# A graph network's tail on one core: the last batch's first 128 columns taken ahead of the rest, with TensorE's order behind them rewritten

## The reference, cut to what matters

```python
# x [16, 512, 128], adj [16, 512, 512]
def L0(x, mask):                       # per batch
    xc = transpose(x)
    h = relu(bn(conv1d(xc, conv1_w)))
    h = bn(conv1d(h, conv2_w, taps=17))
    x_conv = transpose(relu(h + xc))
    s = x @ w_se.T + b_se
    A = exp(-dist(s, s)) * mask        # 512 x 512
    x_nmp = A @ relu(x @ w_msg.T + b_msg)
    gi = concat(x_conv, x_nmp) @ w_ih.T + b_ih
    gh = x @ w_hh.T + b_hh
    r = sigmoid(gi_r + gh_r); z = sigmoid(gi_z + gh_z)
    n = tanh(gi_n + r * gh_n)
    return (1 - z) * n + z * x
def L1(x, adj):                        # five groups of the first 25 nodes
    for g, idx in enumerate(GROUPS):   # sizes 25, 9, 7, 6, 6
        An = normalised(adj[:, idx][:, :, idx])
        h = relu(An @ (x[:, idx] @ W1[g]) + b1[g])          # 128 -> 256
        out_g = relu(An @ (h @ W2[g]) + b2[g])              # 256 -> 128
        fused[:, idx] += softmax(fusion_w)[g] * out_g
    return fused
x = layernorm(x + L0(x, adj))
x = layernorm(x + L1(x, adj))          # L1 is 0 from node 25 on
```

## Time and profile before

| what | value |
|---|---|
| median of 3 runs | 358.56 us |
| profiled execution | 357.92 us |
| its span | 356.1 us |
| TensorE busy | 340.6 us (96%) |
| VectorE busy | 318.2 us (89%) |
| ScalarE busy | 236.7 us (66%) |
| GpSimd busy | 95.0 us (27%) |
| the chain that ended last, by engine | TensorE 77%, VectorE 10%, ScalarE 5%, issue 4% |
| landing of a store of `yoo`, from issue | 2.3 us |

### The profile page before, as it was taken

The page is one execution under the profiler, slowest core; times in us unless marked ns, Lnnn a source line. Parts: engine busy times, 40 slices in busy tenths (PEclk is TensorE's granted clock), DMA queues, the critical chain, the costliest instruction groups (busy, mean ns, idle before and its releaser), DMA issues.

```text
span 356.1 us, 6267 instructions
## 1 busy us (share of the span) xinstructions
PE 340.6 (96%) x1790; PEld 277.0 (78%) x1790; DVE 318.2 (89%) x562; ACT 236.7 (66%) x409; POOL 95.0 (27%) x153
## 2 busy tenths in 40 slices
PE   4989999999999999999999999999999999999894
PEld 1567678976889688977998788968897798866673
DVE  2999999999999999999999899999999999896526
ACT  4382665748856696748674885669684876876760
POOL 4770001503050504131050505040222206062023
PEclk9999999999999999999999999999999999999998
DMA  6914332514043312604161404412260415301101
GB/s 178 327 24 122 111 112 50 165 31 148 24 128 124 101 49 66 206 0 147 39 204 29 147 17 121 135 59 88 55 203 14 147 33 178 96 12 36 29 2 53
DMA packets 30950, 33.95 MB, mean 95 GB/s; under 512 B 4884, under 2 KB 18124, under 8 KB 30932
## 3 DMA queue, kind: packets, MB, share of 16 engines
q1 hardware_dynamic: 30166, 33.55, 31.4%
q10 hardware_dynamic: 766, 0.18, 0.2%
HBM read 24.85 MB, written 4.40 MB: 82 GB/s over the span
## 4 chain that ended last, share of the span: by engine, by line
PE 77%; DVE 10%; ACT 5%; issue 4%; DMA 2%; SPq 0%; DVEq 0%; POOLq 0%; ACTq 0%; POOL 0%
PE p_outer L669 18%; PE ring L669 15%; PE p_middle L669 14%; PE p_r L669 9%; PE p_z L669 8%; PE p_gi L669 6%; PE p_gh L669 5%; PE ring L748 2%; DMA cst<-consts 2%; DVE am L1331 1%; ACT am_h L1101 1%; ACT yoo L1083 1%; ACT ac L376 1%; DVE gtn L1337 1%; ACT he L373 1%
## 5 line engine op out<-in xcount | busy, mean ns | idle before, releaser
L1232 POOL TENSOR_TENSOR base<-mv,vscale 128x4 f32<-128x4 f32 x16 | 5.1, 319 | 235.3 <-DVE mv L1363 235.3
L669 PE MATMUL p_outer<-t_h,w_h 128*128 128x344 f32 x131 | 41.1, 329 | 0.3 <-DVE rz L1445 0.2
L669 PE MATMUL p_outer<-t_h,w_l 128*128 128x344 f32 x131 | 40.3, 323 | 0.6 <-DVE w_l L1448 0.6
L1331 DVE TENSOR_TENSOR am<-am,adj 128x512 f32<-128x512 f32 x64 | 40.0, 684 | 0.0
L1504 DVE TENSOR_TENSOR am_l<-am,am_h 128x2048 fp32r<-128x2048 f32 x15 | 34.3, 2287 | 1.8 <-ACT am_h L1101 1.8
L669 PE MATMUL p_middle<-t_h,w_h 128*128 128x344 f32 x90 | 28.7, 329 | 0.4 <-DVE rz L1454 0.4
L1101 ACT ACTIVATE am_h<-am 128x2048 fp32r<-128x2048 f32 x15 | 28.5, 1902 | 0.0
L669 PE MATMUL p_middle<-t_h,w_l 128*128 128x344 f32 x90 | 28.0, 322 | 0.0
L669 PEld LDWEIGHTS p_outer<-t_h,w_h 128*128 128x128 f32 x131 | 24.4, 188 | 2.6 <-ACT t_h L978 0.7
L1083 ACT ACTIVATE yoo<-yn,nb,rs 128x128 f32<-128x128 f32 x64 | 26.2, 485 | 0.0
L669 PEld LDWEIGHTS p_outer<-t_h,w_l 128*128 128x128 f32 x131 | 24.4, 189 | 1.3 <-DVE w_l L1448 0.9
(11 more groups left out here) (346 smaller groups left out, 1021.3 us busy)
## 6 DMA issues: line engine op xcount, KB each, us to landing
adj<-adjT SPq DMA_DIRECT2D x64, 256.0 KB, 3.3
xpad<-xT SPq DMA_DIRECT2D x17, 256.0 KB, 3.1
out<-yoo SPq DMA_DIRECT2D x16, 256.0 KB, 2.3
crossed<-left SPq DMA_DIRECT2D x31, 48.0 KB
left<-left SPq DMA_DIRECT2D x30, 48.0 KB
right<-left SPq DMA_DIRECT2D x30, 48.0 KB
wc<-w_c SPq DMA_DIRECT2D x2, 384.0 KB, 6.8
wraw<-g_w SPq DMA_DIRECT2D x1, 640.0 KB
```

Of the source, the lines that this page charges most:

```text
L669: return nc.tensor.matmul(out_, w, x, start=start, stop=stop, skip_group_check=True)
L1232: TT(base[:, 0:CH], mv[:, :, 1], vscale[:, 0:CH], ALU.mult)
L1331: TT(am[:, c, :], am[:, c, :], adj[:, c, :], ALU.mult).then_inc(s_am[c], 1)
```

## The change

The last batch's first 128 columns (`HEAD`) go ahead of the other 384 (`REST`) through the gate tanhs, the candidate, the result, one transposition, the copy (into a new tile `y_first`), the statistics and a power of their own (`base_first`, `rs_first`). The 25 rows of `x1` come from these alone. ScalarE's four writes of batch 14 are taken out of the last batch's part, and stand behind `hidden(4)`; its 25 rows stay where they were (`node_share`). TensorE's order becomes: first layer 0, wait for the head's result, head transposition, first layer 1 and 2, second layer 0, wait for `s_grow`, aggregate(2), first layer 3 and 4, three transpositions, second layer 1 and 2, wait for `yn`, first_late, second layer 3 and 4, back, aggregate2(0), second_late, residual, aggregate2(1), scatter(0), aggregate2(2), scatter(1), scatter(2). Two banks change: the third lot's aggregate goes to `ring[1]`, the second half of first_late to `p_middle`. The sync engine's stream is not changed, nor is VectorE's order from `hidden_late` on.

Left out of the diff are the new tiles and semaphores, the names `HEAD, REST = slice(0, D), slice(D, N)`, the split of ScalarE's `normalise` into the four writes (the first of which can read `y_first`) and `node_share`, and VectorE's old `normalise`. The counts mean: `A_RT, A_NN, A_ZT, A_YN = 1, 2, 3, 4`; `V_GG` to `V_MV` = 1 to 7 for gate product, sum, input share, candidate share, result, statistics, aggregate; `G_BASE, G_RS = 1, 2`.

```diff
--- before.py
+++ after.py
...
@@ -260,10 +265,10 @@
         BC_BANKS = MSEL_BANKS = (p_outer, p_middle)
-        TR_BANKS = (p_outer, p_middle, p_z)
+        TR_BANKS = (p_outer, p_middle, ring[1])
         W1_BANKS = (p_outer, p_middle, ring[1], p_gh, p_r, p_z)
         W2_BANKS = (p_gi, p_r, p_z)
-        W1_LATE = (ring[0], p_z)
+        W1_LATE = (ring[0], p_middle)
         W2_LATE = p_gi
         TS_BANKS = (p_outer, p_middle)
         AGG2_BANKS = (ring[1], p_gh, p_r)
...
@@ -318,6 +324,8 @@
                             pe.wait_ge((s_hid0, s_hid1)[k], g - 2)
                         if (g, k) == (1, 1):
                             pe.wait_ge(s_ghb, B)
+                        if (g, k) == (4, 0):
+                            pe.wait_ge(s_agT, 3)
                         mm(cols(W1_BANKS[(2 * g + k) % 6], g), gw1[:, g, D * k:D * k + D],
                            agT[:, ERL, group(g)]).then_inc(s_first, 1)
@@ -928,27 +936,33 @@
             batches(pe, step)
             pe.wait_ge(s_nl, B)
             pe.wait_ge(s_agT, 2); pe.wait_ge(s_gw1d, 16)
-            g_pe.first_early(pe, mm, range(3))
+            g_pe.first_early(pe, mm, range(1))
+            pe.wait_ge(s_head_dve, V_Y2); pe.wait_ge(s_yn, B - 1)
+            nc.tensor.transpose(R_T[:, HEAD], y2[:, HEAD], cst[:, C_ID:C_ID + D]).then_inc(s_t0, 1)
+            g_pe.first_early(pe, mm, range(1, 3))
             pe.wait_ge(s_tt, B)
             g_pe.second_early(pe, mm, range(1))
-            pe.wait_ge(s_y2, B)
-            transposes()
+            pe.wait_ge(s_grow, B); pe.wait_ge(s_hid0, 2)
+            g_pe.aggregate(pe, mm, 2)
             g_pe.first_early(pe, mm, range(3, NG))
-            g_pe.second_early(pe, mm, range(1, NG))
-            pe.wait_ge(s_sT, NG)
+            pe.wait_ge(s_y2, B); pe.wait_ge(s_head_act, A_YN)
+            for c in range(1, CH):
+                last = nc.tensor.transpose(R_T[:, D * c:D * c + D], y2[:, D * c:D * c + D], cst[:, C_ID:C_ID + D])
+            last.then_inc(s_t, 1)
+            g_pe.second_early(pe, mm, range(1, 3))
+            pe.wait_ge(s_yn, B); pe.wait_ge(s_hid1, 4)
+            g_pe.first_late(pe, mm)
+            g_pe.second_early(pe, mm, range(3, NG))
+            pe.wait_ge(s_sT, NG); pe.wait_ge(s_hid1, NG + 1)
             for i in EARLY:
                 g_pe.back(pe, mm, i)
             g_pe.aggregate2(pe, mm, 0)
-            pe.wait_ge(s_grow, B)
-            g_pe.aggregate(pe, mm, 2)
-            g_pe.aggregate2(pe, mm, 1)
-            pe.wait_ge(s_yn, B)
-            g_pe.first_late(pe, mm)
-            g_pe.scatter(pe, mm, 0)
-            g_pe.scatter(pe, mm, 1)
             g_pe.second_late(pe, mm)
             g_pe.residual(pe, mm, 2)
+            g_pe.aggregate2(pe, mm, 1)
+            g_pe.scatter(pe, mm, 0)
             g_pe.aggregate2(pe, mm, 2)
+            g_pe.scatter(pe, mm, 1)
             g_pe.scatter(pe, mm, 2)
@@ -1076,15 +1090,20 @@
                 A(fe[:], fw[:], ACT.Exp, bias=fs[:, 1:2], accum_out=fs[:, 2:3]).then_inc(s_fe, 1)
                 gates(z)
-            def normalise(q, n, k, pair=None):
+            def normalise(q, n, k, pair=None, head=None):
                 after(act, s_nb, n(k + 1)); after(act, s_rs, n(k + 1))
                 act.wait_ge(s_out[q], dma_count(n, q, k))
                 for c in range(CH):
-                    last = A(yo[q][:, c, :], yn[:, c, :], ACT.Identity, bias=nb[:, c:c + 1], scale=rs[:, c:c + 1])
+                    rows_ = head if head is not None and c == 0 else yn[:, c, :]
+                    last = A(yo[q][:, c, :], rows_, ACT.Identity, bias=nb[:, c:c + 1], scale=rs[:, c:c + 1])
                 last.then_inc(s_yo, 1)
                 if pair is not None:
-                    A(x1[SLOT * q:SLOT * q + GN, pair, :], yn[0:GN, 0, :], ACT.Identity, bias=nb[0:GN, CH:CH + 1],
-                      scale=rs[0:GN, CH:CH + 1]).then_inc(s_grow, 1)
+                    node_share(q, n, k, pair)
+
+            def node_share(q, n, k, pair):
+                after(act, s_nb, n(k + 1)); after(act, s_rs, n(k + 1))
+                A(x1[SLOT * q:SLOT * q + GN, pair, :], yn[0:GN, 0, :], ACT.Identity, bias=nb[0:GN, CH:CH + 1],
+                  scale=rs[0:GN, CH:CH + 1]).then_inc(s_grow, 1)
             loop_pair = [None]
@@ -1150,8 +1169,9 @@
                     act.wait_ge(s_ya, B - 1)
                     for i in EARLY:
                         g_act.channels(act, i)
-                    normalise(0, n, -1, PAIRS - 1)
-                gates(n)
+                    node_share(0, n, -1, PAIRS - 1)
+                if more:
+                    gates(n)
             def step(b, v, n):
                 (odd if v % 2 else even)(b, v, n)
@@ -1166,23 +1186,39 @@
             for b in (B - 2, B - 1):
                 step(b, b, Fixed(b))
             last = Fixed(B)
+            act.wait_ge(s_gr, B); act.wait_ge(s_gg, B - 1)
+            A(rt[:, HEAD], p_r[:, HEAD], ACT.Tanh, bias=prm[:, P_RH:P_RH + 1], scale=0.5).then_inc(s_head_act, 1)
+            A(rt[:, REST], p_r[:, REST], ACT.Tanh, bias=prm[:, P_RH:P_RH + 1], scale=0.5).then_inc(s_rt, 1)
+            act.wait_ge(s_head_dve, V_TT); act.wait_ge(s_yb, B - 1)
+            A(nn[:, HEAD], tt[:, HEAD], ACT.Tanh, bias=vec[:, V_IN:V_IN + 1]).then_inc(s_head_act, 1)
+            act.wait_ge(s_gz, B); act.wait_ge(s_ya, B - 1)
+            A(zt[:, HEAD], p_z[:, HEAD], ACT.Tanh, bias=prm[:, P_ZH:P_ZH + 1], scale=0.5).then_inc(s_head_act, 1)
+            A(zt[:, REST], p_z[:, REST], ACT.Tanh, bias=prm[:, P_ZH:P_ZH + 1], scale=0.5).then_inc(s_zt, 1)
             g_act.hidden(act, 0)
-            candidate(last, -1)
+            act.wait_ge(s_t0, 1)
+            A(y_first[:], R_T[:, HEAD], ACT.Copy).then_inc(s_head_act, 1)
+            act.wait_ge(s_tt, B)
+            A(nn[:, REST], tt[:, REST], ACT.Tanh, bias=vec[:, V_IN:V_IN + 1]).then_inc(s_nn, 1)
             g_act.hidden(act, 1)
             g_act.hidden(act, 2)
-            node_rows(last, -1)
+            g_act.channels(act, 2)
+            g_act.support(act, 0)
             g_act.hidden(act, 3)
             g_act.hidden(act, 4)
-            for g in range(NG):
-                g_act.support(act, g)
+            normalise(0, last, -2)
+            act.wait_ge(s_t, B); act.wait_ge(s_yo, B - 1); act.wait_ge(s_grow, B - 1)
+            A(yn[:, 1:CH, :].rearrange("p c d -> p (c d)"), R_T[:, REST], ACT.Copy).then_inc(s_yn, 1)
+            g_act.support(act, 1)
+            g_act.support(act, 2)
+            g_act.hidden_late(act)
+            g_act.support(act, 3)
+            g_act.support(act, 4)
             for i in EARLY:
                 g_act.rows_early(act, i)
-            g_act.channels(act, 2)
             g_act.weigh(act, 0)
+            normalise(1, last, -1, None, y_first[:])
+            g_act.rows_late(act)
             g_act.weigh(act, 1)
-            g_act.hidden_late(act)
-            normalise(1, last, -1)
-            g_act.rows_late(act)
             g_act.weigh(act, 2)
             store_groups(act, 2, 1)
@@ -1260,6 +1296,10 @@
                     TT(dg[:, 3, :], dg[:, 2, :], cst[0:CC, C_MH:C_MH + PAIRS], ALU.pow).then_inc(s_dpow, 1)
             batches(pool, step)
+            pool.wait_ge(s_head_dve, V_MV)
+            TS(base_first[:], mv[:, 0, 1:2], 1.0, 4 * EPS, ALU.mult, ALU.add).then_inc(s_head_pool, 1)
+            pool.wait_ge(s_head_pool, G_BASE)
+            TT(rs_first[:], base_first[:], cst[:, C_MH:C_MH + 1], ALU.pow).then_inc(s_head_pool, 1)
             powers(Fixed(B), -1)
             for i in range(3):
                 groups_power(pool, i)
...
@@ -1564,16 +1597,46 @@
             first()
             batches(dve, step)
-            last = Fixed(B)
-            gate_mid(last, -1)
-            keep_share(B, last, -1)
+            dve.wait_ge(s_head_act, A_RT); dve.wait_ge(s_ghb, B)
+            STT(gg[:, HEAD], rt[:, HEAD], 1.0, gg[:, HEAD], ALU.add, ALU.mult).then_inc(s_head_dve, 1)
+            dve.wait_ge(s_head_dve, V_GG); dve.wait_ge(s_gi, B); dve.wait_ge(s_nn, B - 1)
+            TT(tt[:, HEAD], p_gi[:, HEAD], gg[:, HEAD], ALU.add).then_inc(s_head_dve, 1)
+            dve.wait_ge(s_rt, B)
+            STT(gg[:, REST], rt[:, REST], 1.0, gg[:, REST], ALU.add, ALU.mult).then_inc(s_gg, 1)
+            dve.wait_ge(s_gg, B)
+            TT(tt[:, REST], p_gi[:, REST], gg[:, REST], ALU.add).then_inc(s_tt, 1)
+            dve.wait_ge(s_head_act, A_ZT); dve.wait_ge(s_y2, B - 1)
+            STT(ya[:, HEAD], zt[:, HEAD], 3.0, xin[:, (B - 1) % 4, HEAD], ALU.add, ALU.mult).then_inc(s_head_dve, 1)
+            dve.wait_ge(s_head_act, A_NN)
+            STT(yb[:, HEAD], zt[:, HEAD], -1.0, nn[:, HEAD], ALU.add, ALU.mult).then_inc(s_head_dve, 1)
+            dve.wait_ge(s_head_dve, V_YA); dve.wait_ge(s_head_dve, V_YB); dve.wait_ge(s_t, B - 1)
+            TT(y2[:, HEAD], ya[:, HEAD], yb[:, HEAD], ALU.subtract).then_inc(s_head_dve, 1)
             g_dve.hidden(dve, 0)
-            result(last, -1)
```

(40 more changed lines are left out.)

## The result

The changed kernel takes 364.49 us, the median of 4 runs (362.71 to 366.52); the kernel before took 358.69 beside it. The ratio is 1.0146, 95% interval 1.0091 to 1.0200: slower, clear of noise; whether by less than 2% these runs leave just undecided. The forecast was 360.9 in a range of 358.4 to 363.1. The profiled execution is the lowest of the four: 362.71, span 360.9.

A forecast was written before the change was run, and what follows sets the result against it. The landing of scatter(0), which starts VectorE's final sums, was taken to set the end; 0.93 + 0.64 + 0.29 + 1.16 = +3.0 us gave span 359.1, plus 1.82 around it, 360.9 us, range 358.4 to 363.1.

The forecast's parts named there:

- Ahead of scatter(0): TensorE products moved before scatter(0), 2.59 us; net of the old gap and VectorE's saved wait, +0.93 us without new waits.
- Wait (a): TensorE, after group 0, waits for VectorE's result of the first 128 columns before the head transposition: 0.64 us.
- Wait (b): TensorE waits before aggregate(2) for the 25 node rows, through copy, statistics, power and write: 0.29 us.
- Wait (c): TensorE waits before first_late for ScalarE's 384-column copy, which stands behind the four moved writes: 1.16 us.
- Final chain: VectorE's final sums, from the first scatter's landing to its last instruction: 6.51 us without the wait for the last scatter.
- At no cost: Both new banks, ordinary statistics and powers, last batch's writes, stores and extra instructions: claimed to add nothing where not counted.
- the clock rival: Clock falls to 1.2 GHz behind TensorE's third new wait, adding between nothing and 9.5 us, up to 370.4; chance 0.03.

The follow-up runs named there:

- filled kernel: The change with unread products in TensorE's three new waits: 25.46 us from first layer 0 to VectorE's end, median 362.47 us; filling only the third also gave 25.46.
- order alone: The kernel before with only second_late and the residual put ahead of scatter(0) on TensorE: 24.64 us from first layer 0 to VectorE's end, median 360.41 us, ratio 1.0070.
- rows tile: The change with a separate tile for the last 384 node rows, copied before batch 14's writes: 24.11 us from first layer 0 to VectorE's end, median 360.49 us.
- the change again: The changed kernel itself, unedited, measured once more with six runs: median 364.26 us, ratio 1.0154 against the kernel before.
- waits covered: The change with rows tile, early scatters, second layer 3 and 4 before first_late, first layer 1 and 3 and support(0) earlier: 358.23 us, 0.9962; repeated 358.09 us, 0.9961.

## Why the prediction was wrong

The direction and the mechanism of the sum were right: the end hangs on the landing of scatter(0). At full clock the sum of the steps was 0.3 short, measured by the filled kernel (25.46) against 359.1 - 2.55 - 331.37 = 25.18 forecast.

- *Ahead of scatter(0)*, +0.93 without waits. Its core, 2.59 of products less the 0.28 wait, is 2.31; the order alone, with the old gap left in, measured 2.46.
- *Wait (a)*: head transposition forecast 1.82 after first layer 0, measured 333.56 - 331.82 = 1.74. In part this is luck: the date 333.13 has the three last pieces of VectorE in it with 0.27 each, and not with the 0.33 that the text states; they took 0.28, 0.28 and 0.29. On ScalarE the 128-column tanhs took 0.37 out of PSUM and 0.40 for the candidate, the copy 0.28, where the prediction took 0.34 and the table that it quotes has 0.25.
- *Wait (b)*: aggregate(2) forecast at 4.43, measured 4.56; GpSimd's first instruction took 0.40, not the 0.20 of its neighbours.
- *Wait (c)*: first_late forecast at 8.13, measured 8.41; the wait, 1.16 forecast, is 1.10 in the bracket, and taking its cause away gives 1.35 back. Most of the 0.28 lies here: without (c) the sum is 22.18 + 0.93 + 0.64 + 0.29 = 24.04, and the rows tile measured 24.11.
- *Final chain*: 6.51 forecast, 6.45 measured. *At no cost*: both new banks, the powers, the last writes and the stores did not hold anything up.

**The step that failed is the clock rival**: that a gap "no longer than one that the trace shows harmless should do nothing". By it the clock stood in the sum with nothing, and the rival had a chance of 0.03. Both profiles of the change have a stretch at 1.2 GHz behind the 1.10 us wait before first_late, beginning at 343.9 (first_late began at 340.23) and at 342.4 (340.26). It costs 1.21 us in the one and 2.61 in the other. The profiled span comes out as 359.1 + 0.45 (a later start of the tail) + 0.28 (steps) + 1.21 (clock) - 0.14 (the store's landing) = 360.9. The other one, whose 364.19 is close to both medians, comes out as 359.1 + 0.47 + 0.28 + 2.61 - 0.06 = 362.4; without the 2.61 it would lie inside my range. All ten runs of the change have a mean clock of 0.991 or less (0.978 to 0.991); how much of that lies in the tail is known for the two traced ones only. Filling that wait brings the median from 365.0, with the two short ones filled beside it, to 362.1. The row shows one gap in one execution; it was read as a rule for the kernel. A fifth of the other runs of the kernel before, too, have a clock of 0.991 or less, which one profile could not tell.

The Trainium skill (TensorE: Matmul & The Clock Gate, on the clock gate) has the engine throttled after idleness. The traces agree in that the clock is kept where the wait is filled. But it is kept behind the gap of 1.30 in both traces that have it whole (before, order alone), and falls behind the shorter one of 1.10 in four of four; no run here explains that.

Left open, then: why this gap and not that one. The work behind them differs (twenty short products of 50 columns and less behind the new one, 350 columns behind the old), but no kernel here changed that alone. Nor is it known why the stretch is longer in one execution than in another, or what brings on the low stretches near the start.

## What to carry to other kernels

Find which instruction's landing starts the last chain on another engine, and count what is put in front of it: 2.6 us of products moved ahead of the first scatter cost 2.5 us, though each engine's total work stayed the same. When a step is taken early, look at what it has to overtake: here four writes of the batch before, hidden until then, ended up in front of a copy because both used one tile. And a TensorE wait costs more than its own length when the clock falls behind it. One profile shows one draw, so compare many runs; but look up in the trace where the clock was low before you put a low mean down to a gap.

## What the runs showed that was not expected

The clock doesn't fall in the 1.10 us gap but 2.1 to 3.7 us after its end: in the first profile of the change at the end of a short wait of 0.33 (343.9 to 347.3), in the second in the midst of work (342.4 to 349.2), and it comes back while that work goes on. The same program shows low stretches in other places from one execution to the next: the change again has one from 21.5 to 24.9 that its first profile doesn't have, and "waits covered" one from 13.0 to 16.5 that its repetition doesn't have. Filling most of a single gap of 1.30 us in the kernel before changed nothing that can be seen (3 low runs of 12, against 20 of 89).
